# A twelve-layer decoder in one kernel: norm statistics taken in the stage in front, and routed tokens fetched by lists and added by diagonal products

## The chip, the cores and the metric

The kernel runs on one core of a Trainium2 chip, in float32 throughout. The metric is the device time of one execution in microseconds (us), taken as the median of several runs. The engines are TensorE (PE in the profile, its weight loads PEld), VectorE (DVE), ScalarE (ACT), GpSimd (POOL) and SyncE (SP), which here issues most DMAs.

## The reference

A stream x of 16 sequences with 112 tokens of 256 channels passes four layers of three sub-layers each; every sub-layer reads a layer norm of x and is added to x.

```python
m = mean(x); v = var(x); _layernorm = (x - m) / sqrt(v + eps)
x = x + L0_attn(_layernorm(x))         # rwkv-like recurrence
x = x + L0_xattn(_layernorm(x), ctx)   # cross attention, 16 heads, context 375 rows of 192
x = x + L0_ffn(_layernorm(x))          # one dense MLP
x = x + L1_attn(_layernorm(x))         # long convolution, then a second norm and a gated MLP
x = x + L1_xattn(...); x = x + L1_ffn(...)   # 8 experts, two picks per token
x = x + L2_attn(...);  x = x + L2_xattn(..., mask); x = x + L2_ffn(...)  # 8 experts again
x = x + L3_attn(...);  x = x + L3_xattn(...); x = x + L3_ffn(...)        # 4 fixed experts
# the routed one:
topk_val, topk_idx = top_k(logits, 2); scores = softmax(topk_val)
out_e = silu(a) * g @ W2[e] + b2[e]            # for every expert e
out = sum(out_e[topk_idx] * scores)            # over the two picks
```

## The kernel before

x stays on chip as `X` (112 tokens on the partitions, 16 batches of 256 columns, "b" below); `XT` is its normalised transpose. Each sub-layer is a row of blocks, and a block ends when all engines in it have ended, so work of one block does not overlap that of the next, except for what SP has issued. Semaphores order the engines within a block; each engine runs its instructions in the order of the code.

`layer_norm` (L158 on) takes `bn_stats` of eight batches (L206), aggregates them (L209), adds epsilon (L212), lets GpSimd take the power -1/2 (L259), does the same for the other eight, and then VectorE normalises batch by batch (L239), TensorE transposes (L270) and ScalarE copies to `XT`. There is one such norm at the head of each of the twelve sub-layers and a second in L1_attn. The batches of X that it reads were added just before: by `project_out` (L1951, two batches a round), by the attention loop's "O" job (L1369), by `feed_forward` (L417, L419) or by `gather_results` (L987, L989).

`context_attention` (L0_xattn, L1_xattn, L2_xattn) runs a loop over batches and groups of four heads. Between the scores (L1247), the transposes of the probabilities (L1227) and the weighted sums (L1270), TensorE does one "job" at a time, all in PSUM bank 6: per batch K for two column halves (L1189), V for three row tiles (L1199), Q (L1194) and the output O (L1214). The 192 context channels are two chunks of 96 rows. A job waits until VectorE has copied out the one before it.

`sub_l3_xattn` works directly on the context, loading per batch `keys` and `rows` (281 KB each) into three slots; both slots are given free when the batch's weighted sum is done.

A routed MLP: `router` makes the gates; `place_tokens` computes for each token and pick a slot in an array sorted by expert; `add_second_biases` adds the gated second biases to X on VectorE (L569) while GpSimd sends all tokens by 32 indirect DMAs (`scatter_tokens`, L785) to `rows_in` in HBM; `expert_tiles` runs 35 tiles of 128 rows, for each of which SP loads rows (L832), loads the expert's first weights (L837) and stores the result to `rows_out` (L843), TensorE transposes (L872) and multiplies (L884, L893); `gather_results` fetches two rows per token by 32 indirect DMAs (L978), and VectorE multiplies and adds them (L987, L989). At the program's start ScalarE's queue writes zeros over `rows_in`. `KT` is 128, `T` 112, `GB` 4 batches a group, `G` 4 groups, `PICKS` 2.

## Time and profile before

| what | value |
|---|---|
| time, median of 3 runs (range) | 3467.72 us (3465.84 to 3471.27) |
| the profiled execution: its own time, its span | 3473.44 us, 3471.7 us |
| TensorE matmul busy | 2742.4 us, 79% |
| VectorE, ScalarE, GpSimd busy | 1504.5, 1278.5, 870.4 us |
| mean granted TensorE clock | 0.88 |

The sub-layers lie one behind the other. By the windows read from the trace they end at: L0_attn 319, L0_xattn 685, L0_ffn 854, L1_attn 1199, L1_xattn 1620, L1_ffn 1970, L2_attn 2122, L2_xattn 2516, L2_ffn 2922, L3_attn 3094, L3_xattn 3222, L3_ffn 3463 us; then X is stored. A busy share over the whole span says little here; each stage has its own limit, and what is read is which engine waits in it, for what, and how long. In a timeline row, the number in brackets is the engine's idle time before the row and what ended it.

### The profile page before, as it was taken

The numbers are of one execution on the slowest core, as the hardware profiler recorded it, in microseconds if no ns is written. First come the engines' busy times: TensorE is split into PE (matmuls) and PEld (weight loads), VectorE is DVE, ScalarE is ACT, GpSimd is POOL, SyncE is SP. The second block draws the span as 40 slices with busy tenths as digits, with TensorE's granted clock in tenths as the row PEclk, the third lists the DMA queues.
The fourth block names the chain that finished last, engine by engine and source line by source line (L and its number), as shares of the span: only waits on it lengthen the run. The fifth ranks groups of instructions, "written<-read, shape, count | busy, mean of one in ns | idle before, by whom it ended". The sixth has DMA issues, their size and how long they took to land. (4 is left out here: it accounts for less than half of the span.)

```text
span 3471.7 us, 57030 instructions
## 1 busy us (share of the span) xinstructions
PE 2742.4 (79%) x18341; PEld 1973.1 (57%) x18342; DVE 1504.5 (43%) x3582; ACT 1278.5 (37%) x3781; POOL 870.4 (25%) x557
## 2 busy tenths in 40 slices
PE   6554999778786899998399377988848992987798
PEld 2343677545463555554299244666627992865465
DVE  5676888722623333334222484555440004552311
ACT  1322777621531123333022123666613331861111
POOL 2342455400001022222300362444430005320000
PEclk8776999879888999998599687999958996998899
DMA  3000000000330000001276301000035552003000
GB/s 108 1 1 22 17 13 13 6 25 14 77 74 25 33 13 12 12 11 53 84 236 234 108 0 39 12 13 13 5 137 173 181 181 86 1 29 87 26 24 21
DMA packets 116639, 192.75 MB, mean 56 GB/s; under 512 B 57715, under 2 KB 91714, under 8 KB 104754
## 3 DMA queue, kind: packets, MB, share of 16 engines
q1 hardware_dynamic: 105634, 171.84, 15.6%
q0 software_dynamic: 6144, 14.69, 1.4%
q10 hardware_dynamic: 4752, 4.85, 0.4%
q8 instruction: 59, 0.97, 0.1%
q14 instruction: 50, 0.41, 0.0%
HBM read 167.92 MB, written 23.43 MB: 55 GB/s over the span
## 5 line engine op out<-in xcount | busy, mean ns | idle before, releaser
L1177 POOL TENSOR_TENSOR L_xattn_p<-L_xattn_p,L_xattn_ri 112x1500 f32<-112x1500 f32 (+1 forms) x192 | 435.8, 2270 | 655.0 <-DVE L_xattn_ri L1380 655.0
L1307 ACT ACTIVATE L_xattn_pT<-ps 125x448 f32<-125x448 f32 (+1 forms) x576 | 254.9, 476 | 385.6 <-PE ps L1227 385.2
L1319 ACT ACTIVATE L_xattn_p<-L_xattn_sa,L_xattn_ng 112x375 f32<-112x375 f32 x512 | 304.8, 598 | 68.6 <-DVE L_xattn_ng L1409 48.5
L1227 PEld LDWEIGHTS ps<-ident,L_xattn_p 112*125 112x125 f32 x1920 | 259.9, 191 | 88.6 <-issue 19.6
L1227 PE MATMUL ps<-ident,L_xattn_p 112*125 112x112 f32 x1920 | 284.6, 279 | 14.7 <-POOL L_xattn_p L1177 8.8
L270 PE MATMUL ps<-ident,ln_xn 112*128 112x112 f32 x416 | 99.0, 399 | 241.4 <-DVE ln_xn L239 222.9
L884 PE MATMUL ps<-L_ffn_xsT,L_ffn_w 128*128 128x128 f32 x2240 | 267.5, 279 | 11.3 <-issue 10.0
L884 PEld LDWEIGHTS ps<-L_ffn_xsT,L_ffn_w 128*128 128x128 f32 x2240 | 266.6, 195 | 15.9 <-issue 12.5
L259 POOL TENSOR_TENSOR ln_rstd<-ln_tmp,ln_half 112x8 f32<-112x8 f32 x26 | 45.8, 1763 | 793.8 <-DVE ln_tmp L212 602.8
L270 PEld LDWEIGHTS ps<-ident,ln_xn 112*128 112x128 f32 x416 | 67.1, 211 | 274.0 <-issue 246.1
L1199 PE MATMUL ps<-L_xattn_pack,L_xattn_src 97*125 97x256 f32 (+3 forms) x576 | 198.4, 468 | 30.5 <-DVE L_xattn_v L1359 29.9
L1189 PE MATMUL ps<-L_xattn_src,L_xattn_pack 96*128 96x375 f32 x512 | 202.4, 521 | 22.9 <-DVE L_xattn_kT L1340 16.6
L941 DVE COPY L_ffn_y<-ps 128x256 f32<-128x256 f32 x70 | 29.7, 425 | 393.7 <-PE ps L893 393.7
L893 PE MATMUL ps<-L_ffn_weights,L_ffn_hT 128*128 x840 | 192.9, 379 | 2.2 <-DVE L_ffn_hT L952 2.2
L978 POOL DMA_INDIRECT L_ffn_got<-rows_out,slot x64 | 59.9, 935 | 504.7 <-PEq L971 485.8
L1247 PE MATMUL ps<-L_xattn_kT,L_xattn_qm 32*112 32x375 f32 (+1 forms) x1280 | 173.1, 523 | 3.7 <-DVE L_xattn_ng L1406 1.8
L379 PE MATMUL ps<-L_ffn_w,L_ffn_h 128*112 128x256 f32 x768 | 169.0, 379 | 0.0
L367 PE MATMUL ps<-XT,L_ffn_w 128*128 x384 | 151.6, 551 | 20.0 <-DMA L_ffn_w<-in_L_ffn_experts 20.0
L914 ACT ACTIVATE L_ffn_xsT<-ps 128x256 f32<-128x256 f32 x72 | 27.6, 383 | 378.5 <-PE ps L872 378.5
L893 PEld LDWEIGHTS ps<-L_ffn_weights,L_ffn_hT 128*128 128x128 f32 x840 | 154.2, 190 | 20.9 <-issue 2.8
L419 DVE SCALAR_TENSOR_TENSOR X<-ps,L_ffn_gates,X 112x256 f32 x80 | 33.2, 477 | 299.6 <-PE ps L379 299.6
L379 PEld LDWEIGHTS ps<-L_ffn_w,L_ffn_h 128*112 128x112 f32 x768 | 135.9, 177 | 36.0 <-issue 7.7
(378 smaller groups left out, 5069.7 us busy)
## 6 DMA issues: line engine op xcount, KB each, us to landing
L_ffn_w<-in_L_ffn_experts SPq DMA_DIRECT2D x74, 1024.0 KB, 5.1
L_xattn_src<-in_ctx SPq DMA_DIRECT2D x48, 281.2 KB, 2.9
L_attn_toeplitz<-L_attn_h SPq DMA_DIRECT2D x4, 3136.0 KB, 23.4
L_ffn_xs<-rows_in SPq DMA_DIRECT2D x74, 128.0 KB, 2.2
rows_out<-L_ffn_y SPq DMA_DIRECT2D x70, 128.0 KB, 2.3
L_ffn_weights<-in_L_ffn_experts SPq DMA_DIRECT2D x8, 1028.0 KB, 14.7
rows_in<-zeros ACTq DMA_DIRECT2D x1, 4736.0 KB, 27.2
L_xattn_keys<-in_ctx SPq DMA_DIRECT2D x16, 281.2 KB, 3.0
```

What stands on the lines that cost most here:

```text
L270: last = pe.transpose(k.ps[0:KP, u, c * T:(c + 1) * T], xn[:, u, c * KP:(c + 1) * KP], k.ident[0:T, 0:T])
L367: last = pe.matmul(k.ps[0:rows, bank, 0:GT], w1[s][:, c, col:col + rows], src[:, c, bass.ds(g * GT, GT)], start=(c == 0), stop=(c == 1))
L379: last = pe.matmul(k.ps[0:T, 4 + j, 0:D], hT[:, h, m, j * T:(j + 1) * T], w2[s][:, m, :], start=(m == 0), stop=(m == hidden - 1))
L884: last = pe.matmul(k.ps[:, 2 * u + half, j * KT:(j + 1) * KT], w1[:, u, c, at:at + KP], xT[:, u, c, :], start=(c == 0), stop=(c == 1))
L893: last = pe.matmul(k.ps[:, 6 + u, 0:D], hT[:, u, m, :], weights[:, bass.ds(e * rest + (o2 + m * D), D)], start=(m == 0), stop=(m == hidden ...
L1177: g.tensor_tensor(P[:, m % 4, :, :], P[:, m % 4, :, :], ri[:, m % 4, :].unsqueeze(2).broadcast_to([T, W, S2]), ALU.mult).then_inc(s["prob_ ...
L1189: last = pe.matmul(k.ps[:, bank, 0:S2], wk[0:kr, kc, c * KP:(c + 1) * KP], src[0:kr, u, kc, :], start=(kc == 0), stop=(kc == 1))
L1199: last = pe.matmul(k.ps[0:KW, bank, 0:HD], src[0:rows, u, kc, c * KW:(c + 1) * KW], wv[0:rows, kc, :], start=(kc == 0), stop=(kc == 1))
L1227: last = pe.transpose(turned(t)[:, j * T:(j + 1) * T], P[:, m % 4, j, kc * KW:(kc + 1) * KW], k.ident[0:T, 0:T])
L1247: last = pe.matmul(scores(n)[:, j, :], qm[rows, u, e, c, :], KT[rows, u, c, :], start=True, stop=True)
L1307: act.activation(PT[:, m % 4, kc, :, :].rearrange("p h t -> p (h t)"), turned(t), ACT.Copy).then_inc(s["pt_ev_a"].sem, 1)
L1319: last = act.activation(P[:, n % 4, j, :], at, ACT.Exp, bias=ng[:, n % 4, j:j + 1], scale=-1.0 if mask else 1.0, accum_out=rs[:, n % 4, j: ...
```

## The change

Seven parts.

1. `bn_stats` moves out of `layer_norm` into the stage in front: right behind the addition that completes a batch of X, VectorE waits for that addition and takes the batch's statistics into a tile that lives for the whole program. `layer_norm` only aggregates. The first norm takes them as quarters of X land. The dense MLPs, all attentions and the gather do so; L3_ffn, the last, has no norm behind it.
2. The routed MLPs no longer scatter. The normalised tokens are written once, in order, to `rows_x`; `add_second_biases` also computes on VectorE and TensorE, for every tile, the list of its rows; GpSimd fetches each tile's rows by list from `rows_x` and sends its results by list to `rows_y`, where they lie by token and pick. SP loads weights alone.
3. The gather becomes eight plain DMAs of 448 KB on the queues of SP and ScalarE. ScalarE makes, ahead of the tiles, 32 diagonal matrices `shares` from the picks' weights; TensorE multiplies each fetched block by its matrix and sums the two picks in PSUM; VectorE adds the sums to X, two batches at a time.
4. In L2_xattn the context is laid out as 128 rows and 64 rows, the 64 held twice. K's two halves form one job, V's tiles 0 and 1 form one, V's tile 2 is made in two column halves: the 64-row products of each pair lie in two different row groups of TensorE. A batch has five jobs, not seven, and a pair fills banks 6 and 7.
5. L3_xattn has four slots for `keys`, free when the scores are done, and five for `rows`.
6. X is stored in four quarters, each when its last addition is done.
7. X is loaded in four quarters and the first weights are issued right behind them; 3712 KB of zeros are written, not 4736.

```diff
+    def moments(self, v, b, of=None):
+        of = self.X if of is None else of
+        return v.bn_stats(self.st[:, bass.ds(6 * b, 6)], of[:, bass.ds(b * D, D)])
...
@@ project_out, behind the two additions of a round @@
+                    for u in range(2):
+                        b = 2 * i + u
+                        v.wait_ge(*s["res_done"].at(b + 1))
+                        k.moments(v, b, of=out)
...
@@ add_second_biases @@
+                def list_rows(c):
+                    pe.wait_ge(*s["rg_hot"].at(c + 1))
+                    for n in range(c * part, (c + 1) * part):
+                        last = pe.matmul(k.ps[0:KT, 6, 0:2 * (most - 1)], place[:, n, :],
+                                         owned[:, n, :, :].rearrange("p w q -> p (w q)"), start=(n == 0),
+                                         stop=(n == picks - 1))
...
@@ expert_tiles @@
-                        load(t + 2, 1 - u)
-                        load_first(t + 2, 1 - u)
-                        store(t - 1, u)
+                        load_first(2 * i + u + 3, 1 - u)
...
+                def fetch(t):
+                    g.wait_ge(*s["rg_turned"].at(t - 1))
+                    g.indirect_dma_start(xs[:, t % 2, :], None, k.rows_x[:, :],
+                                         bass.IndirectOffsetOnAxis(ap=route.rows[:, 0, t:t + 1], axis=0)).then_inc(
+                                             x_in[t % 2].sem, 16)
+                def send(t):
+                    g.wait_ge(*s["rg_y"].at(t + 1))
+                    g.indirect_dma_start(k.rows_y[:, :],
+                                         bass.IndirectOffsetOnAxis(ap=route.rows[:, 1, t:t + 1], axis=0),
+                                         y[:, t % 2, :], None).then_inc(y_out[t % 2].sem, 16)
+                for t in range(NT):
+                    if t + 2 <= NT:
+                        fetch(t + 2)
+                    if t > 0:
+                        send(t - 1)
...
+                for n in range(PICKS):
+                    for b in range(B):
+                        act.activation(shares[:, n, b, :], k.ident[0:T, 0:T], ACT.Copy,
+                                       scale=route.weight[:, n, b:b + 1])
...
@@ gather_results, with parts = 8 and per = 2 @@
-                    for n in range(PICKS):
-                        g.indirect_dma_start(got[:, b % ring, n * D:(n + 1) * D], None, rows[:, :],
+                    eng.dma_start(got[:, q * per:(q + 1) * per, :, :], rows[:, q * per:(q + 1) * per, :, :]).then_inc(
+                        into[q % 4].sem, 16)
...
+                            last = pe.matmul(k.ps[0:T, q % 4, u * D:(u + 1) * D], shares[:, n, q * per + u, :],
+                                             got[:, q * per + u, n, :], start=(n == 0), stop=(n == PICKS - 1))
...
+                    v.tensor_tensor(x, k.ps[0:T, q % 4, 0:per * D], x, ALU.add).then_inc(s["rg_added"].sem, 1)
+                    if q > 0:
+                        look(q - 1)
...
@@ context_attention @@
+    if paired:
+        places = {(0, "a"): ("K", 0), (0, "b"): ("V", 2), (1, "a"): ("O", 0), (1, "b"): ("Q", 0), (3, "b"): ("V", 0)}
...
+                if kind == "K" and paired:
+                    for c in range(C):
+                        pe.matmul(k.ps[:, bank + c, 0:S2], wk[:, 0, c * KP:(c + 1) * KP], src[:, u, 0, :], start=True,
+                                  stop=False)
+                    for c in range(C):
+                        rows = slice(64 * c, 64 * c + 64)
+                        last = pe.matmul(k.ps[:, bank + c, 0:S2], wk[rows, 1, c * KP:(c + 1) * KP], src[rows, u, 1, :],
+                                         start=False, stop=True)
...
@@ sub_l3_xattn @@
-    SLOTS = 3
+    KS, RS = 4, 5
...
-                sp.wait_ge(*summed.at(b - SLOTS + 1))
-                load(sp, b)
+                sp.wait_ge(*scored.at(b - KS + 1))
+                load_keys(sp, b)
+                if b + 1 < B:
+                    sp.wait_ge(*summed.at(b + 1 - RS + 1))
+                    load_rows(sp, b + 1)
```

How instructions stand now. First VectorE in the round of `project_out` in L0_attn, before: `po_x` is the product that the next round's transposes need, `X<-ps,X` one batch's addition; an ISA row is a wait or a signal.

```order
L2275 ISA
L2275 TENSOR_TENSOR po_x<-L_attn_V,L_attn_G 112x256
L1949 ISA
L1951 ISA
L1951 TENSOR_TENSOR X<-ps,X 112x256
L1949 REGISTER_ALU
L1951 ISA
L1951 TENSOR_TENSOR X<-ps,X 112x256
L1932 REGISTER_ALU
```

The same place in the changed kernel.

```order
L2501 ISA
L2501 TENSOR_TENSOR po_x<-L_attn_V,L_attn_G 112x256
L2171 ISA
L2173 ISA
L2173 TENSOR_TENSOR X<-ps,X 112x256
L2171 REGISTER_ALU
L2173 ISA
L2173 TENSOR_TENSOR X<-ps,X 112x256
L122 ISA
L122 BN_STATS st<-X 112x6
L122 ISA
L122 BN_STATS st<-X 112x6
```

Two waits and two statistics now stand at the round's end, in front of the next round's `po_x`.

Second, TensorE in the loop of L2_xattn, before: a K job (L1189), transposes of probabilities (L1227), the other K job.

```order
L1189 MATMUL ps<-L_xattn_src,L_xattn_pack 128x375 x2
L1224 REGISTER_ALU
L1225 REGISTER_ALU
L1227 MATMUL ps<-ident,L_xattn_p 125x112 x4
L1225 REGISTER_ALU
L1227 MATMUL ps<-ident,L_xattn_p 125x112 x4
L1208 REGISTER_ALU
L1189 MATMUL ps<-L_xattn_src,L_xattn_pack 128x375 x2
```

And now: L1330 is the pair's 128-row products, L1334 its two 64-row products in two row groups, L1340 and L1344 the same of V's tile 2 by column halves.

```order
L1330 MATMUL ps<-L_xattn_src,L_xattn_pack 128x375 x2
L1334 MATMUL ps<-L_xattn_src,L_xattn_pack 128x375 x2
L1390 REGISTER_ALU
L1391 REGISTER_ALU
L1393 MATMUL ps<-ident,L_xattn_p 125x112 x4
L1391 REGISTER_ALU
L1393 MATMUL ps<-ident,L_xattn_p 125x112 x4
L1369 REGISTER_ALU
L1340 MATMUL ps<-L_xattn_pack,L_xattn_src 125x128 x2
L1344 MATMUL ps<-L_xattn_pack,L_xattn_src 125x128 x2
```

Both K halves stand in the first job, and V's tile 2 took the place of the second.

Third, VectorE in the routed MLP between `place_tokens` and the tiles, before.

```order
L772 CAST expert<-owner 1x37
L696 UNCONDITIONAL_BRANCH
L564 UNCONDITIONAL_BRANCH
L566 COPY gates_in_order<-L_ffn_gates 112x128
L569 TENSOR_TENSOR X<-ps,X 112x512 x8
L537 UNCONDITIONAL_BRANCH
```

And now: `past`, `rest` and `owned` mark each token's tile and id, `place` its row in the tile; `rows` is the list.

```order
L641 COPY gates_in_order<-L_ffn_gates 112x128
L621 TENSOR_TENSOR past<-pick,L_ffn_pack 112x1184
L623 TENSOR_REDUCE rest<-past 112x32
L624 TENSOR_SCALAR rest<-rest 112x32
L625 TENSOR_TENSOR rest<-rest,pick 112x32
L626 TENSOR_TENSOR past<-past 112x32x36
L616 TENSOR_TENSOR X<-ps,X 112x512 x2
L631 TENSOR_TENSOR owned<-past,L_ffn_pack 112x32x36 x2
L637 TENSOR_TENSOR place<-rest,L_ffn_pack 112x1024
...
L657 SCALAR_TENSOR_TENSOR spare<-ps,L_ffn_pack 128x36
L658 CAST rows<-ps 128x36
L659 TENSOR_TENSOR rows<-ps,spare 128x36
```

The additions of the second biases stand between the steps of the list, and the tiles' first fetch comes behind all of it.

## Rows read from the trace of the kernel before

**Rows 1.** Windows by stage: length; busy PE, PEld, DVE, ACT, POOL; clock; DMA share, GB/s.

```profile
322.00:687.50 365.50, 328.17 (x3360) 242.01 (x3360) 290.17 (x436) 257.74 (x739) 186.73 (x71) 0.96 0.06 16
...
2122.00:2518.00 396.00, 331.38 (x3360) 244.38 (x3360) 206.40 (x779) 257.72 (x740) 178.88 (x68) 0.95 0.06 17
...
3096.00:3224.00 128.00, 92.67 (x448) 66.38 (x448) 39.73 (x120) 27.47 (x90) 5.67 (x4) 0.86 0.28 78
```

**Rows 2.** Timeline where one sub-layer ends and the next begins (start, duration).

```profile
2120.48 1.42 DVE L417 TENSOR_TENSOR X<-ps,X 112x256 f32 x4 [5.06 <-PE ps L379]
...
2122.43 2.71 DVE L206 BATCH_NORM_STATS2 ln_st<-X 112x6 f32<-112x256 f32 x8
...
2126.10 1.65 POOL L259 TENSOR_TENSOR ln_rstd<-ln_tmp,ln_half 112x8 f32<-112x8 f32 x1 [40.47 <-DVE ln_tmp L212]
...
2129.43 3.62 DVE L239 TENSOR_SCALAR ln_xn<-X,ln_mv,ln_rstd 112x256 f32<-112x256 f32 x7
```

**Rows 3.** Timeline of TensorE in the output projection of L0_attn.

```profile
299.22 0.74 PE L1967 MATMUL ps<-ident,po_x 112*128 112x112 f32 x4 [1.25 <-DVE po_x L2275]
...
302.98 0.74 PE L1967 MATMUL ps<-ident,po_x 112*128 112x112 f32 x4 [1.24 <-DVE po_x L2275]
```

**Rows 4.** Timeline of TensorE in L2_xattn, one batch.

```profile
2325.32 1.13 PE L1199 MATMUL ps<-L_xattn_pack,L_xattn_src 96*125 96x256 f32 x4 [1.19 <-DVE L_xattn_v L1359]
...
2326.80 0.90 PE L1247 MATMUL ps<-L_xattn_kT,L_xattn_qm 32*112 32x375 f32 x8
...
2331.20 1.53 PE L1189 MATMUL ps<-L_xattn_src,L_xattn_pack 96*128 96x375 f32 x4 [1.18 <-DVE L_xattn_kT L1340]
...
2337.86 1.14 PE L1194 MATMUL ps<-XT,L_xattn_pack 128*128 x8 [0.68 <-DVE X L1369]
...
2347.85 1.13 PE L1199 MATMUL ps<-L_xattn_pack,L_xattn_src 96*125 96x256 f32 x4 [1.19 <-DVE L_xattn_v L1359]
```

**Rows 5.** Waits in L3_xattn, and the window over its 16 batches.

```profile
PE ps L1808 <- DMA L_xattn_keys<-in_ctx: 20.4, 11, 2.7
...
3117.60:3221.50 103.90, 80.59 (x392) 57.50 (x392) 24.34 (x64) 20.23 (x70) 0.00 (x0) 0.90 0.26 73
```

**Rows 6.** Timeline in L1_ffn, between routing and the first tile.

```profile
1673.28 0.27 DVE L566 COPY gates_in_order<-L_ffn_gates 112x128 f32<-112x128 f32 x1 [0.39 <-PEq L696]
...
1718.76 0.69 PE L872 MATMUL ps<-ident,L_ffn_xs 128*128 128x128 f32 x2 [28.09 <-remote]
...
1719.34 0.34 SPq L837 DMA_DIRECT2D L_ffn_w<-in_L_ffn_experts  x1
...
1724.55 2.26 PE L884 MATMUL ps<-L_ffn_xsT,L_ffn_w 128*128 128x128 f32 x9 [5.10 <-issue]
```

**Rows 7.** VectorE on 4096 elements a partition (timeline, L0_attn).

```profile
283.30 4.42 DVE L2259 TENSOR_TENSOR L_attn_V<-L_attn_V,L_attn_gw 112x4096 f32<-112x4096 f32 x1
```

**Rows 8.** Windows of L1_ffn: its tile loop, and its gather.

```profile
1719.00:1928.00 209.00, 197.45 (x1472) 188.73 (x1471) 54.28 (x175) 54.97 (x177) 0.06 (x1) 0.97 0.68 230
...
1928.00:1973.00 45.00, 0.00 (x0) 0.00 (x0) 18.00 (x41) 0.20 (x1) 29.80 (x32) 0.51 0.32 90
```

**Rows 9.** Timeline of L1_ffn's gather.

```profile
1924.40 0.42 DVE L941 COPY L_ffn_y<-ps 128x256 f32<-128x256 f32 x1 [2.17 <-PE ps L893]
...
1927.94 0.96 POOL L978 DMA_INDIRECT L_ffn_got<-rows_out,slot  x1 [214.06 <-PEq L971]
...
1969.56 0.48 DVE L989 SCALAR_TENSOR_TENSOR X<-L_ffn_got,weight,X 112x256 f32<-112x256 f32 x1
```

**Rows 10.** DMA issues: count, size of one, median time to landing.

```profile
L_ffn_w<-in_L_ffn_experts SPq DMA_DIRECT2D x74, 1024.0 KB, 5.1
...
L_ffn_xs<-rows_in SPq DMA_DIRECT2D x74, 128.0 KB, 2.2
...
X<-in_x SPq DMA_DIRECT2D x1, 1792.0 KB, 10.4
...
out<-X SPq DMA_DIRECT2D x1, 1792.0 KB, 7.9
```

More of the change, by code:

```diff
@@ L176, in layer_norm @@
         tmp = sb("ln_tmp", [T, B])
-        half = sb("ln_half", [T, B])
         xn = sb("ln_xn", [T, 4, D])
@@ L292, in layer_norm, with feed_forward @@
                   rstd_done=4 if two_pows else 2, norm_done=B, norm_tr=B, norm_ev=B)
-def feed_forward(k, name, dram, layout, experts, rows, hidden, gated, act_fn, gates=None, src=None):
+def feed_forward(k, name, dram, layout, experts, rows, hidden, gated, act_fn, gates=None, src=None, out=None):
     nc = k.nc
@@ new lines, in own_rows, with places @@
+                def own_rows():
+                    for w in range(2):
+                        last = v.tensor_tensor(owned[:, :, w, :], past[:, :, 0:most - 1],
+                                               along(ids[:, w * picks:(w + 1) * picks], most - 1), ALU.mult)
+                    ch.link(last)
+                def places(c):
+                    at = slice(c * part, (c + 1) * part)
+                    v.tensor_tensor(place[:, at, :], along(rest[:, at], KT),
+                                    ranks.unsqueeze(1).broadcast_to([T, part, KT]), ALU.is_equal).then_inc(
+                                        s["rg_hot"].sem, 1)
@@ L590, in sub_ffn @@
     elay, edram = packs[name + "_experts"]
-    feed_forward(k, name, edram, elay, spec["experts"], KP, spec["hidden"], spec["gated"], spec["act"], gates)
+    feed_forward(k, name, edram, elay, spec["experts"], KP, spec["hidden"], spec["gated"], spec["act"], gates,
+                 out=k.aps["out"] if spec["mode"] == "fixed" else None)
 def fixed_gates(k, gates, b2):
@@ L995, in sub_routed_ffn @@
+                look(parts - 1)
+        k.advance(rg_added=parts, rg_summed=parts, **{f"rg_got{r}": 32 for r in range(4)})
 def sub_routed_ffn(k, ctx, name, packs, spec):
@@ L1369, in job @@
                     v.tensor_tensor(k.x(b - 2), k.ps[0:T, 6, 0:D], k.x(b - 2), ALU.add).then_inc(job_out.sem, 1)
+                    v.wait_ge(*job_out.at(count))
+                    k.moments(v, b - 2)
+                    return
+                if paired and (kind, c) == order[J_V]:
+                    v.wait_ge(*s["pv_mm"].at((b - 1) * (UB // E)))
+                    store(kind, c, u, 6)
                     return
@@ L3148, in _ @@
             def _(v):
+                v.memset(k.half[:, :], -0.5)
                 v.memset(routed_zeros[:, :], 0.0).then_inc(k["vec_step"].sem, 1)
```

431 lines of the change are left out of this document (292 added, 139 removed).

## The prediction

> **What bounds the kernel now.** I read the windows by sub-layer first. TensorE has the largest busy share in every stage [rows 1], but not all of it: L2_xattn spends 331 of 396 us in products, L3_xattn 93 of 128. So the question in each stage is what TensorE waits for, and I went on to timelines where it stands still. Four kinds of gaps show.
>
> At each sub-layer's start nothing runs but VectorE: the first statistics begin at 2122.43 and the first normalised batch at 2129.43, 7.0 us later [rows 2]. GpSimd's power had ended at 2127.75; VectorE was then still at the statistics of the second eight batches. Inside L2_xattn, TensorE waits three times a batch for VectorE to clear PSUM bank 6: 1.19, 1.18 and 0.68 us of a period of 22.5 [rows 4]. In L3_xattn it waits 11 times for the context, 20.4 us [rows 5]. In a routed MLP it stands still from the router to the first tile (the scatter, 28 us) and again for the whole gather [rows 6, 8, 9]. In between, the tile loop is full: PE is busy 197 of 209 us at a clock of 0.97 [rows 8].
>
> **The change part by part.** *Statistics (part 1).* The norm's statistics leave its head. What stays before the first normalised batch is the aggregation and epsilon (from the end of the statistics at 2125.14 to the power's start at 2126.10, 0.96 us), the power (1.65) and about 0.1 of handover: 2.7 instead of 7.1 with the memset that goes too, so 4.4 us are saved [rows 2]. There are 13 norms; the first is counted below, 12 give 52.8 us. What they cost in front: one statistic is 2.71 / 8 = 0.34 us, with its wait for the addition 0.44. Behind a stage's last addition stand one in the four cross attentions (0.5), four in the three dense MLPs (1.5), two in three output projections (0.8): 2 + 4.5 + 2.4 = 8.9 us. Inside the stages, `project_out` is a chain: TensorE's transposes wait 1.25 us for `po_x`, which VectorE makes behind the two additions, and the period is 302.98 - 299.22 = 3.76 us [rows 3]. The order now puts two waits and two statistics in front of that `po_x`, about 0.75 us in each of 7 rounds: 5.2 us in L0_attn and 5.2 in L1_attn; in L3_attn I count nothing, as that projection lies in a loop with many more products per batch; if it is a chain too, it is 5.2 more, which the lower bound has room for. In L0_xattn VectorE is busy 290 of 365 us [rows 1], so statistics in front of a maximum may delay the softmax; 16 times 0.44 is 7 us at worst, nothing at best; I take 2. Sum 52.8 - 8.9 - 10.4 - 2 = **32 us**. Bounds: 20 (L0_xattn's 7 in full, and 0.5 at every other stage's rounds) and 42 (project_out's share hidden).
>
> *Pairs in L2_xattn (part 4).* A K job of four instructions takes 1.53 us, a V job 1.13 [rows 4]; 3.06 and 3.39 a batch. Of a K pair's eight instructions four are 64-row ones which can run two at a time, so a quarter of the time goes; V's likewise: 0.77 + 0.85 = 1.6 us, and as records overlap their successors a little I take 1.4. That groups of rows do run together is seen in the scores: eight instructions of 375 columns on 32 rows take 0.90 us, where four of 375 columns take 1.53 [rows 4]. The handovers of bank 6 go from seven to five. The wait between V's last two jobs (1.19) has no successor, since V's tile 2 has gone to the other end; the one behind K stays (1.18) and may grow by one copy of 0.55, as the pair has two banks to copy out. So 0.6 to 1.2 us of waits go. Together 2.0 to 2.6, times 16: **35 us**. Bounds 15 (only the matmul time, and that less what follows under the rivals) and 45.
>
> The Trainium skill, page "TensorEngine Tiling (Array Packing)", Key Properties, says that tiles in different row groups work in parallel, with which the row of the scores agrees, but also that changing the tiling mode drains the engine, which speaks against this part. What a change of mode can cost at most is in the same row: ideal for the eight score instructions, at 1.53 / 4 = 0.38 each and four at a time, is 0.77 us; the row has 0.90, so 0.13 remain for a change. The change adds six of these a batch, 0.8 us, 12 us in all.
>
> *L3_xattn (part 5).* Keys are now asked for when a batch's scores are done, four batches ahead, and no longer after the weighted sum of three batches ago. A load of 281 KB is short against a batch's cycle of (103.9 - 25) / 16 = 4.9 us, so the 20.4 us of waits should go. The granted clock of those 104 us was 0.90 [rows 5]: a fifth of the time, 21 us, stood at the lower of its two levels (1.2 of 2.4 GHz), which costs half of it, 10 us; about half of that falls into the waits themselves, so I count 5 more. **25 us**, bounds 14 (the DMAs go on being late every other time) and 29.
>
> *Routed MLPs (parts 2 and 3), twice.* Before, 51.3 us lie between the copy of the gates (1673.28) and the first product (1724.55) [rows 6]. Now the list ends the block. VectorE works through 2 x 1184 + 1152 + 2 x 1152 + 4 x 1024 = 9920 elements a partition (marks and sum, differences, ids, places), at 4.42 us for 4096, or 1.08 ns each [rows 7], 10.7 us; the eight additions of biases are 512 elements from PSUM, 5.3 us; small ones and waits 2; the last list products and the list itself some 3. That makes 21 us. Behind it come a block change (0.4), the fetch (0.96 to issue [rows 9], 2.2 to land [rows 10]), and the first weights, 5.1 us from their issue, as before 1719.34 to 1724.55 [rows 6, 10]: with the diagonal matrices' 32 small copies on ScalarE (estimated at 0.22 us each, 7 us) beside them, the first product at about 29.2. That saves 22.1 us. If VectorE's broadcast operands cost double, 12 less; if the matrices push the first tile, 3 less. The gather before runs from 1924.40 to the end of the last addition at 1970.04, 45.6 us [rows 9], most of it the pitch of GpSimd's issues. Now: copy 0.4, last send 3.3, block change 0.4, 3584 KB at the rate of the output's store (1792 KB in 7.9 us, of which about 2 are fixed [rows 10]), 14 us; the last block's four products, addition and two statistics 3.3. That makes 21.5; I take 22 saved of the possible 24. At the rate of the input's load (10.4 us [rows 10]) it would be 19.4 us of transfer and 18.5 saved. The tile loop I take as unchanged, since TensorE fills it [rows 8]; GpSimd needs two issues of some 1.2 us a tile of 5.5. Both routed MLPs have this code before and after the tiles, so 2 x (22.1 + 22) = **88 us**, bounds 65 and 100.
>
> *Ends (parts 6 and 7).* Instead of 7.9 us for the whole store one quarter remains, (7.9 - 2) / 4 + 2 = 3.5: 4.4 us. The start gains 2: its statistics overlap with the landing of X, but the weights then bound it.
>
> **Sum**: 32 + 35 + 25 + 88 + 4.4 + 2 = 186 us. The profiled execution took 3473.4 us, the median is 5.7 lower; 3473.4 - 186 = 3287, and for the median 3467.7 - 186 = 3282.
>
> **The rivals.** (a) *The lists slow the tiles.* Each tile's rows come by GpSimd's queue, the fetch of one behind the send of another, and TensorE waits at the transposes. For it: in all 32 issues of the old gather GpSimd managed one in 1.24 us. Against: a fetch is asked for two tiles before it is used, 11 us, and needs 3.2. At 1 us a tile for 70 tiles the time is 3282 + 70 = 3352. Chance 0.08. (b) *Pairing and statistics give little*: the 12 us of mode changes, the copy behind the K pair in full, and statistics that delay the maxima in L2_xattn too. Then part 4 gives 15 and part 1 20: 3282 + 20 + 12 = 3314. For it: TensorE already waits for VectorE in just that loop. Chance 0.14. (c) *The plain gather runs no faster per byte than the indirect one*, whose window shows 90 GB/s and a DMA share of 0.32 [rows 8]: 41 us instead of 14 a gather, and 3282 + 54 = 3336. Against: the low rate goes with the issues' pitch. Chance 0.06. (d) *Slower than before*: the fetch needs more than its 11 us. It decides from 186 / 70 = 2.7 us a tile, so 13.7 us from request to landing, over four times the rows' 3.2; at 16 us the time is 3282 + 5 x 70 = 3632. Nothing speaks for it but that the trace has no indirect fetch beside full weight traffic (DMA share 0.68). Chance 0.02. (e) *More than I count*: the granted clock, 0.86 in L3_xattn and 0.90 in its loop [rows 1, 5], lies between its two levels wherever TensorE had stood idle, and may rise at more places than L3_xattn as gaps close: some 30 us, 3250. Chance 0.10. My forecast has 0.60.
>
> **The numbers.** The independent errors (about 11, 13, 7 and 17 us of the four large parts) make 25 us around 3282 for the likeliest case; with (b) and (e) within and most of (a) and (d) without, 3246 to 3330. A measurement of this kernel tells about 0.2%, 7 us. All cases but (d) are faster by far: 0.97, and 0.01 for no change.
>
> **What would show it.** Right: first normalised batch 2.7 us after a norm's block begins; no wait for `keys`; first tile product about 29 us behind the gates' copy; from the last tile's copy to the next norm 22 us; the L2_xattn period 20.2 us; project_out's period 4.5. Wrong: a wait of TensorE for `xs` in the tile loop, a period over 21 us in L2_xattn with its waits for VectorE grown, or a list block over 25 us.

## The result

| kernel | median, us | ratio to before, 95% interval |
|---|---|---|
| before | 3468.26 | |
| changed | 3344.91 | 0.9644 (0.9627 to 0.9660) |

The change takes 123 us off, 3.6%. I had forecast 186 and a range of 3246 to 3330; the time lies above it. The page of the changed kernel begins:

```profile
span 3343.8 us, 57353 instructions
...
PE 2799.0 (84%) x18661; PEld 1999.5 (60%) x18662; DVE 1519.8 (45%) x3568; ACT 1294.2 (39%) x3845; POOL 888.0 (27%) x570
```
The profiled spans differ by 127.9 us. Cut at the first normalised batch of each norm, they fall to the stages so (worked out from the timelines of both; a stage holds the head of the next norm):

| stage | before | changed | difference | forecast |
|---|---|---|---|---|
| to the first norm | 24.3 | 27.0 | +2.8 | -2 |
| L0_attn | 302.4 | 308.6 | +6.2 | +1.6 |
| L0_xattn | 365.6 | 368.2 | +2.7 | -1.9 |
| L0_ffn, L1_attn | 514.1 | 507.5 | -6.6 | -4.2 |
| L1_xattn | 421.5 | 415.8 | -5.6 | -3.9 |
| L1_ffn, L2_ffn | 756.6 | 696.6 | -60.0 | -96.8 |
| L2_attn, L3_attn | 323.5 | 315.7 | -7.8 | -6.5 |
| L2_xattn | 393.5 | 368.1 | -25.4 | -38.9 |
| L3_xattn | 127.7 | 99.9 | -27.8 | -28.9 |
| L3_ffn and the store | 242.5 | 236.2 | -6.3 | -4.4 |

(The forecast column is the prediction's terms, each norm's 4.4 us less its tail put to the stage in front.) The forecasts sum to -186, the spans to -128. Of the missing 58 us 37 are in the two routed MLPs; the rest is in L2_xattn, L0_attn, L0_xattn and the start.

**What came as forecast.** The head of a norm, here L3_xattn's, in the timeline of the changed kernel:

```profile
3004.20 0.43 DVE L122 BATCH_NORM_STATS2 st<-X 112x6 f32<-112x256 f32 x1
...
3005.01 0.64 DVE L217 BATCH_NORM_AGGREGATE ln_mv<-st 112x2 f32<-112x6 f32 x8 [0.38 <-PEq L1697]
...
3005.93 3.44 POOL L267 TENSOR_TENSOR ln_rstd<-ln_tmp,half 112x8 f32<-112x8 f32 x2 [9.22 <-DVE ln_tmp L220]
...
3007.62 4.71 DVE L247 TENSOR_SCALAR ln_xn<-X,ln_mv,ln_rstd 112x256 f32<-112x256 f32 x7 [1.02 <-POOL ln_rstd L267]
```
The statistics of the last batch (L122) end before the block; aggregation, power and first normalised batch follow each other, 2.6 us where [rows 2] has 7.0. L3_xattn's waits for keys are gone, and its stage is 28 us shorter where I had said 29. The store at the end is one quarter.

**Start.** The timeline of the changed kernel:

```profile
7.54 11.96 ACTq L3385 DMA_DIRECT2D rows_x<-zeros  x1
...
19.97 0.35 SPq L198 DMA_DIRECT2D L_attn_pack<-in_L_attn  x1
...
27.02 3.29 DVE L247 TENSOR_SCALAR ln_xn<-X,ln_mv,ln_rstd 112x256 f32<-112x256 f32 x9
```
ScalarE's second DMA issue, one row of zeros, takes 12.0 us, behind the 3712 KB that it issued at 7.06. The block ends with it: SP issues the next one's first DMA at 19.97. X's statistics, meant to overlap with its landing, begin only then.

**L0_attn's projection.** VectorE's product, TensorE's transposes and the window of the changed kernel:

```profile
297.51 0.76 DVE L2501 TENSOR_TENSOR po_x<-L_attn_V,L_attn_G 112x256 f32 x2
...
298.07 0.74 PE L2193 MATMUL ps<-ident,po_x 112*128 112x112 f32 x4 [1.86 <-DVE po_x L2501]
...
303.23 0.76 DVE L2501 TENSOR_TENSOR po_x<-L_attn_V,L_attn_G 112x256 f32 x2
...
290.30:332.90 42.60, 29.34 (x96) 19.71 (x96) 18.10 (x48) 5.92 (x17) 0.00 (x0) 0.70 0.00 0
```
And the same projection in the kernel before:

```profile
288.30:319.50 31.20, 21.98 (x96) 15.00 (x96) 12.94 (x32) 5.92 (x18) 0.00 (x0) 0.92 0.00 0
```
TensorE waits 1.86 us for `po_x`, 0.6 more than in [rows 3]. The round that starts at 297.51 ends at 303.23, 5.7 us and not 4.5; of the five rounds behind the first two, one (303.23 to 307.60) takes 4.4 us, the others 5.6 to 6.2, and the eight product records in them take 3.0 to 3.6 us together, not 2.0. The projection takes 42.6 us after 31.2, 11.4 more where I had 6.0, and the granted clock over it is 0.70 after 0.92: the other 5.4 us are the clock. In L1_attn's projection, the same loop, a round takes 4.11 us after 3.54 and TensorE waits 1.69 us after 1.12, and there the clock of the rounds stays at 1.00. So longer waits went with a lower clock in L0_attn (1.82 to 1.86 us of 4.4) and not in L1_attn (1.69 of 4.1); what lies between the two, no run here tells.

**L2_xattn.** TensorE in the changed kernel:

```profile
2275.69 1.13 PE L1340 MATMUL ps<-L_xattn_pack,L_xattn_src 128*125 128x256 f32 x4
...
2276.75 0.70 PE L1344 MATMUL ps<-L_xattn_pack,L_xattn_src 64*125 64x256 f32 x4
...
2278.83 1.53 PE L1330 MATMUL ps<-L_xattn_src,L_xattn_pack 128*128 128x375 f32 x4
...
2280.28 0.90 PE L1334 MATMUL ps<-L_xattn_src,L_xattn_pack 64*128 64x375 f32 x4
...
2281.11 1.13 PE L1393 MATMUL ps<-ident,L_xattn_p 112*125 112x112 f32 x8
...
2282.85 0.70 PE L1340 MATMUL ps<-L_xattn_pack,L_xattn_src 128*125 128x128 f32 x4 [0.61 <-DVE L_xattn_kT L1518]
...
2283.48 0.49 PE L1344 MATMUL ps<-L_xattn_pack,L_xattn_src 64*125 64x128 f32 x4
...
2246.47 1.14 PE L1355 MATMUL ps<-XT,L_xattn_pack 128*128 x8 [0.68 <-DVE X L1560]
...
2267.93 1.14 PE L1355 MATMUL ps<-XT,L_xattn_pack 128*128 x8 [0.66 <-DVE X L1560]
```
From Q job to Q job it is 21.5 us after 22.5 [rows 4]; I had forecast 20.2. K's pair is 1.53 + 0.90 = 2.43 us after 3.06, V's tiles 0 and 1 are 1.13 + 0.70 = 1.83 after 2.26. But tile 2 in halves of 128 columns is 0.70 + 0.49 = 1.19 us after 1.13. And the transposes of the probabilities got slower, in the groups by line over 12 batches, changed kernel first, then before.

```profile
L1393 PE MATMUL ps<-ident,L_xattn_p 112*125 112x112 f32 x575 | 84.9, 283 | 4.2 <-ACT L_xattn_pT L1475 4.2
```

```profile
L1227 PE MATMUL ps<-ident,L_xattn_p 112*125 112x112 f32 x576 | 78.8, 273 | 0.0
```
They cost 6.1 us more in 12 batches, 0.5 a batch: eight of them take 1.13 us behind 64-row products (2281.11) and 1.02 behind the 96-row ones of before. That is three of the five groups that got slower; the other two stand where a job has gone, one behind the scores and one behind a wait. TensorE's busy time over 12 batches is 236.1 of 257.5 us after 234.7 of 270.3: it did not fall at all. Records overlap, so the sizes are better read from start to start. A K job of the kernel before is 1.37 us long by that:

```profile
2327.63 1.53 PE L1189 MATMUL ps<-L_xattn_src,L_xattn_pack 96*128 96x375 f32 x4
...
2329.00 1.02 PE L1227 MATMUL ps<-ident,L_xattn_p 112*125 112x112 f32 x8
```
Two of them took 2.74 us, and the pair takes 2.28 (2278.83 to 2281.11). All five jobs of a batch took 5.55 us, and the three pairs take 5.03. These 0.5 us are what the transposes give back. TensorE's waits fell, for bank 6 and the like from 35.4 to 22.1 us, 1.1 us a batch, and that is the whole gain.

**The lists and the first tile**, L1_ffn of the changed kernel, and the window of its lists' block:

```profile
1672.61 0.27 DVE L641 COPY gates_in_order<-L_ffn_gates 112x128 f32<-112x128 f32 x1 [0.38 <-PEq L789]
...
1684.33 3.69 PE L582 MATMUL ps<-owned,place 112*128 112x72 f32 x16 [1.16 <-DVE place L637]
...
1706.41 0.18 DVE L659 TENSOR_TENSOR rows<-ps,spare 128x36 int32<-128x36 f32 x1
...
1708.43 1.20 POOL L937 DMA_INDIRECT L_ffn_xs<-rows_x,rows  x1 [48.85 <-issue]
...
1716.05 0.69 PE L967 MATMUL ps<-ident,L_ffn_xs 128*128 128x128 f32 x2 [10.02 <-DMA L_ffn_xs<-rows_x,rows]
...
1717.21 0.93 PEld L979 LDWEIGHTS ps<-L_ffn_xsT,L_ffn_w 128*128 128x128 f32 x4 [0.88 <-ACT L_ffn_xsT L1009]
...
1672.60:1705.00 32.40, 30.91 (x109) 24.21 (x109) 17.18 (x20) 2.13 (x4) 0.00 (x0) 0.50 0.00 1
```
From the gates' copy to the list it is 34.0 us (I had 21), to the first tile product 44.6 (I had 29.2; before, 51.3 [rows 6]). VectorE is busy 17 of 32 us, as costed; TensorE is busy 31 of them, at a granted clock of 0.50, the lower level of 1.2 GHz, from end to end. In L2_ffn it is the same, 34.0 and 44.4 us. Then the first fetch takes from 1708.43 to 1716.05 to be used, 7.6 us and not 3.2. The tile loop itself, from the first tile product to the last result's copy, takes 199.5 us after 199.9.

**The gather**, same place:

```profile
1920.32 8.86 SPq L1078 DMA_DIRECT2D L_ffn_got<-rows_y  x4
...
1925.80 16.44 PE L1098 MATMUL ps<-L_ffn_got,L_ffn_shares 112*112 112x256 f32 x64 [9.16 <-DMA L_ffn_got<-rows_y]
...
1942.88 1.39 DVE L122 BATCH_NORM_STATS2 st<-X 112x6 f32<-112x256 f32 x4
...
1944.65 0.64 DVE L217 BATCH_NORM_AGGREGATE ln_mv<-st 112x2 f32<-112x6 f32 x8 [0.37 <-PEq L1072]
```
From the last result's copy (1916.67) to the next norm it is 28.0 us after 46.2 (1924.40 [rows 9] to the next norm's first statistics at 1970.58); I had 21.5. The loads took about 16 us (their DMA share is 1.13 to 1.14 until 1935). TensorE's 64 instructions, of which I had counted only the last eight, take 16.4 us and begin 5.5 us behind the loads' issue, at a clock of 0.50 until 1930.

### The profile page after: what moved, and what is told of

Its sections match the earlier page's. It is cut to its first block and busy times, and to the rows that moved or that the text cites. A ratio compares the mean times of both kernels' runs of the same rounds, so it can differ in the third digit from the quotient of the medians.

```text
span 3343.8 us, 57353 instructions
## 1 busy us (share of the span) xinstructions
PE 2799.0 (84%) x18661; PEld 1999.5 (60%) x18662; DVE 1519.8 (45%) x3568; ACT 1294.2 (39%) x3845; POOL 888.0 (27%) x570
## 3 DMA queue, kind: packets, MB, share of 16 engines
q8 instruction: 62, 1.02, 0.1%
## 5 line engine op out<-in xcount | busy, mean ns | idle before, releaser
L1393 PEld LDWEIGHTS ps<-ident,L_xattn_p 112*125 112x125 f32 x1920 | 253.1, 190 | 115.4 <-ACT L_xattn_pT L1475 35.4
L1393 PE MATMUL ps<-ident,L_xattn_p 112*125 112x112 f32 x1920 | 294.7, 284 | 21.2 <-ACT L_xattn_pT L1475 11.3
L267 POOL TENSOR_TENSOR ln_rstd<-ln_tmp,half 112x8 f32<-112x8 f32 x26 | 44.3, 1720 | 785.4 <-DVE ln_tmp L220 596.3
L411 ACT ACTIVATE L_ffn_h<-ps,L_ffn_w 128x448 f32<-128x448 f32 x96 | 60.8, 633 | 251.2 <-PE ps L382 251.2
L1360 PE MATMUL ps<-L_xattn_pack,L_xattn_src 96*125 96x256 f32 (+3 forms) x384 | 145.9, 503 | 11.7 <-DVE L_xattn_v L1550 11.1
L1350 PE MATMUL ps<-L_xattn_src,L_xattn_pack 96*128 96x375 f32 x384 | 147.4, 508 | 6.1 <-DVE L_xattn_kT L1528 2.1
L943 POOL DMA_INDIRECT rows_y<-L_ffn_y,rows x70 | 69.2, 988 | 293.8 <-DVE L_ffn_y L1041 287.3
```

The source lines that it names most:

```text
L1350: last = pe.matmul(k.ps[:, bank, 0:S2], wk[0:kr, kc, c * KP:(c + 1) * KP], src[0:kr, u, kc, :], start=(kc == 0), stop=(kc == 1))
L1360: last = pe.matmul(k.ps[0:KW, bank, 0:HD], src[0:rows, u, kc, c * KW:(c + 1) * KW], wv[0:rows, kc, :], start=(kc == 0), stop=(kc == 1))
L1393: last = pe.transpose(turned(t)[:, j * T:(j + 1) * T], P[:, m % 4, j, kc * KW:(kc + 1) * KW], k.ident[0:T, 0:T])
```

## The experiments

Ratios are to the kernel before on the same chip, with their intervals; "us" is the difference to the changed kernel's 0.9644, at 3468 us. Those intervals are some 6 us wide to either side, so a difference of two ratios under about 8 us is not told from nothing. "Stage" numbers are from the profiled executions, one each, cut as in the table above. Stages that an edit leaves alone differ from profile to profile: L0_attn 305.2 to 310.6 us, L1_attn's first part 190.2 to 195.0, L0_xattn 366.7 to 372.5, L1_ffn 318.1 to 320.1, the others by 1 to 3 us.

**Statistics back in the norms** (e1). `layer_norm` takes `bn_stats` as before, all `moments` in front are gone.

```diff
-                    if x_in is not None:
-                        for b in range(h * HB, (h + 1) * HB):
+                    for b in range(h * HB, (h + 1) * HB):
...
-                            last = k.moments(v, b)
+                        last = k.moments(v, b, of=src)
...
-                    v.wait_ge(*job_out.at(count))
-                    k.moments(v, b - 2)
```

> All statistics are back at the head of each norm (part 1 undone; the other parts stay; the waits for a batch's own addition go too). Theory from the two traces: each of 12 norms gets 4.4 us longer (53), and the stages in front get back what the statistics cost there: about 10 us in L0_attn, 5 in L1_attn, 5 to 7 in L0_xattn, 7 of tails elsewhere. Part 1 is then worth some 26 us: 3371. My prediction's term of 32 would give 3377. Rival, that the statistics cost in front as much as they give behind: 3345.

Ratio 0.9689 (0.9673 to 0.9705), +16 us; the profiled span is 24 longer. Part 1 is worth 16 to 24 us. By stages: L0_attn is 6.6 us shorter without it, L0_xattn 2.8 and L3_xattn 1.4; L1_attn, L2_attn, L3_attn, L1_xattn, L2_xattn and the MLPs that have a norm behind them are 2 to 5.4 longer each. In L0_xattn the norm behind the stage accounts for 4.4 us the other way, so the 16 statistics in that loop cost about 2.8 + 4.4 = 7.2 us, near my upper bound; with this stage's scatter it is anything from 5.6 to 11.5.

**Statistics one round later in project_out** (e5).

```diff
+                begin(0)
+                begin(1)
+                finish(0)
+                with v.Fori(1, B // 2 - 1) as i:
+                    begin(i + 1)
+                    look(i - 1)
+                    finish(i)
...
```

> In project_out VectorE takes a round's two statistics one round later, behind the next round's po_x and ahead of the additions, where it waits for products anyhow; nothing else changes. Theory: the 0.75 us a round were on the chain because they stood ahead of po_x, and in L0_attn they also let the granted clock fall (0.69 over the projection, 0.90 before). Both go: L0_attn 8 us shorter, L1_attn's first part 4, so 3346 - 12 = 3334. Rival, that the chain runs through the additions in any place: no change.

Ratio 0.9627 (0.9607 to 0.9648), -6 us, within the intervals; the profiled span is 12.0 shorter. The stages are plain: L0_attn is 9.0 us shorter, L1_attn's first part 4.9, both below every profile with the old place. TensorE in L0_attn:

```profile
302.79 0.74 PE L2204 MATMUL ps<-ident,po_x 112*128 112x112 f32 x4 [1.29 <-DVE po_x L2512]
...
306.57 0.74 PE L2204 MATMUL ps<-ident,po_x 112*128 112x112 f32 x4 [1.26 <-DVE po_x L2512]
...
290.00:324.50 34.50, 22.16 (x96) 15.15 (x96) 20.26 (x58) 6.12 (x18) 0.00 (x0) 0.89 0.00 0
```
The wait is 1.29 us as before the change, the period 3.78, the clock 0.89; in L1_attn the round is back at 3.54 us. From the first `po_x` to the next norm's first instruction on VectorE the projection of L0_attn takes 31.6 us, where it was 42.6 in the changed kernel and 31.3 before. The statistics' place, not their length, cost what the two stages gained here, some 14 us give or take their scatter.

**Statistics behind the maxima in the attentions** (e6): the pair of `wait_ge` and `moments` goes to the end of the step.

> In the three context attentions VectorE takes the statistics of an O job at the end of its step, behind the maxima and the step's other jobs, and no longer between the addition and the maxima. Theory: L0_xattn loses its 4 to 5 us, 3341; L1_xattn and L2_xattn within 1 us of before. Rival, that L0_xattn is full on VectorE, and 16 times 0.43 us cost the same anywhere: 3346.

Ratio 0.9635 (0.9618 to 0.9653), -3 us, which the intervals don't tell from nothing. The stage tells a little more: L0_xattn took 365.6 us here, and 361.3 and 362.9 in e11 and e14b, which have other edits too; in eleven profiles with the changed kernel's order it took 366.7 to 372.5. So the edit gains something there, 1 to 7 us by this run; the scatter allows no closer figure.

**The small DMA first** (e4): the issue for `rows_x` stands ahead of the one for `rows_y`.

> At the start ScalarE issues the small DMA (one row of zeros to rows_x) before the large one, not behind it. In the changed kernel the second issue kept ScalarE for 12.0 us and with it the block until 19.97. Theory: the block ends at about 8, statistics run as X lands, and the first normalised batch comes at 18 to 21 instead of 27; the weights' load then bounds L0_attn's start, so 5 to 7 us of the time, 3339. Rival, that the DMA engines are full with X and zeros and nothing comes earlier: 3345.

Ratio 0.9623 (0.9606 to 0.9639), -7 us, at the edge of what the intervals tell. The timeline is plain:

```profile
7.05 0.51 ACTq L3382 DMA_DIRECT2D rows_x<-zeros  x1
...
7.60 0.42 ACTq L3383 DMA_DIRECT2D rows_y<-zeros  x1
...
20.45 5.84 DVE L247 TENSOR_SCALAR ln_xn<-X,ln_mv,ln_rstd 112x256 f32<-112x256 f32 x16
```
Both issues now take 0.5 us, and the first normalised batch comes 6.6 us earlier. L0_attn is 1.2 us longer, which is less than its scatter.

**L2_xattn unpaired** (e2) and **paired in one row group** (e12).

```diff
-    paired = mask
+    paired = False
...
@@ e12, for K, and the same for V @@
-                        rows = slice(64 * c, 64 * c + 64)
+                        rows = slice(0, 64)
```

> L2_xattn alone goes back to seven jobs a batch and 96-row products (part 4 undone). By the trace of the changed kernel a batch takes 21.1 us instead of 22.5, so 16 batches cost 22 us more: 3367. The prediction's term (35) would give 3380; the rival that pairing saves only matmul time, 0.65 us a batch, and no waits, 3355.

> In L2_xattn both 64-row products of a pair read rows 0 to 63, one row group (the 64 channels stand there twice, so the result is the same). Theory: in the changed kernel they overlap almost fully, at 0.83 us for K's four instructions against 1.45 us for the four of 128 rows; one behind the other they take 1.4 to 1.5 us, so K + 0.6, V tiles 0 and 1 + 0.4, V tile 2 + 0.2 per batch, times 16: 3346 + 19 = 3365. Rival, that what they gain is the handover and not the overlap: 3350.

e2: 0.9697 (0.9681 to 0.9714), +18 us, its stage 17.9 longer. e12: 0.9696 (0.9680 to 0.9712), +18 us, its stage 15.2 longer. TensorE of e12, K's pair:

```profile
2267.05 1.53 PE L1330 MATMUL ps<-L_xattn_src,L_xattn_pack 128*128 128x375 f32 x4
...
2268.50 1.52 PE L1334 MATMUL ps<-L_xattn_src,L_xattn_pack 64*128 64x375 f32 x4
```
In one row group the four 64-row instructions take 1.52 us, as long as four of 128 rows; in two they take 0.90 (above), of an ideal of 0.76. The overlap is worth 15.2 us, 0.95 us a batch; without it 2.7 of the 17.9 us of stage time are left, which the whole times don't tell from nothing.

The Trainium skill, "TensorEngine Tiling (Array Packing)", Key Properties, says both that tiles work in parallel and that a change of mode drains the engine. The trace agrees with the first (1.52 against 0.90), and fits the second. The starts of single instructions show what a change costs. Products of 375 columns follow each other every 0.315 us, of 128 rows as of 64 in e12; from the last one of 128 rows to the first of 64 it is 0.41, and from that to the next 0.42. Behind the 64-row products it is the same: 0.09 us more up to the first transpose, and 0.20 from it to the second, where 0.10 to 0.11 is usual. So each change of row count costs 0.09 + 0.10 = 0.19 us, in e12 without any overlap as in the changed kernel with it, and in the kernel before wherever TensorE leaves the 32-row scores. It is not a cost of 64-row products as such, since in e12 they run at the pace of the others behind the first. Two transposes behind a wait, when TensorE was empty, also start 0.20 us apart, which fits a drain.

The six changes that the pairs add are then 1.1 us a batch, 18 in the stage, and not the 0.8 and 12 that the prediction gave to rival (b): its row of the scores holds only the half of a change that falls inside the group. Without them the three pairs would take 4.15 us where the five jobs took 5.55, just the 1.4 us that the prediction counted; this last is worked out, no run removes the changes alone.

**L3_xattn with three slots** (e3).

```diff
-    KS, RS = 4, 5
+    KS, RS = 3, 3
...
-                sp.wait_ge(*scored.at(b - KS + 1))
+                sp.wait_ge(*summed.at(b - KS + 1))
```

> L3_xattn has three slots for keys and rows again, both free after the weighted sum (part 5 undone). Theory: the 20 us of waits for keys and the slower clock behind them come back, 3345 + 25 = 3370. Rival, that the load time and not the slots made the waits: no more than 5 us, 3350.

Ratio 0.9726 (0.9710 to 0.9742), +28 us; the stage is 28.6 longer, and the waits (here for eight of the batches, in the window up to 3110 us) are back:

```profile
PE ps L2021 <- DMA L_xattn_keys<-in_ctx: 14.7, 8, 2.7
```

**TensorE warmed up for the lists** (e7). In `place_tokens`, nine products whose result nobody reads:

```diff
+                for _ in range(9):
+                    pe.matmul(k.ps[:, 7, 0:512], k.ident[:, :], k.XT[:, 0, 0:512], start=True, stop=True)
```

> During place_tokens, where TensorE has nothing to do for 11 us, it runs nine products of 128 rows and 512 columns into a bank that nobody reads; the lists' block behind it is unchanged. Theory A: the list block (34 us) is bound by TensorE at the lower clock (granted 0.50 throughout, busy 31 of 32 us), because it had stood idle before; started at the full clock it halves until VectorE's 20 us bound it: 14 us saved in each routed MLP, 3318. Theory B: the small products (8 rows, or 72 columns) don't hold the clock, it is back at 0.50 within a few us, and no more than 3 us are saved each time: 3341.

Ratio 0.9653 (0.9635 to 0.9670), no difference. Windows of the lists' block:

```profile
1672.00:1676.00 4.00, 2.40 (x20) 1.95 (x21) 3.48 (x6) 1.80 (x4) 0.00 (x0) 1.00 0.00 0
...
1676.00:1680.00 4.00, 2.23 (x9) 1.47 (x8) 3.86 (x7) 0.00 (x0) 0.00 (x0) 0.83 0.01 2
...
1685.00:1690.00 5.00, 5.00 (x17) 4.03 (x17) 1.23 (x2) 0.00 (x0) 0.00 (x0) 0.50 0.00 0
```
The block starts at the full clock (1.00), but is back at 0.50 within 8 us, in which TensorE is busy 4.6 us, and stays there while TensorE is busy 5.00 of 5 us. Theory A is wrong: standing idle before is not what keeps the clock low. With this block's products, of 8 rows or of 72 columns, it doesn't come up again, though TensorE is full; in the gather, with products of 112 rows and 256 columns, it rises from 0.50 to 1.00 within some 5 us. Which trait of the products decides, no run here separates.

**Less, and other, work on TensorE in the lists' block** (e9, e13b). e9 moves the gates' transposes and four of eight pairs of bias products into `place_tokens`; e13b on top makes the other four ahead of the list products, while VectorE marks.

```diff
-                for c in range(4):
-                    if route is not None:
-                        list_rows(c)
-                    if c < 2:
-                        biases(4 + 2 * c)
-                        biases(5 + 2 * c)
+                for i in range(4, 8):
+                    biases(i)
+                for c in range(4 if route is not None else 0):
+                    list_rows(c)
```

> The gates' transposes, their copies and the first four of eight pairs of bias products (24 of TensorE's instructions and their clock-bound 10.3 us) move from the lists' block forward into place_tokens, where TensorE has nothing to do for 11 us; the additions stay in the lists' block. Theory: that block is bound by TensorE at the lower clock, so it gets 9 to 10 us shorter in each routed MLP: 3346 - 19 = 3327. Rival, VectorE's chain of marks and places bounds it at about 30 us: at most 3 us each, 3340.

> On e9_early_bias: in the lists' block VectorE first adds the four pairs of biases that are ready, then makes marks and places; TensorE makes the other four pairs of bias products (7.4 us) under the marks and then the list products without a break. Theory: the block is the sum of VectorE's head (the trace of e9: 9.8 us, now with 1.3 more) and of TensorE's work behind the first place; with 7.5 us of that moved under the head, the block takes 11 + 14.8 + 0.5 = 26 us instead of 32 in e9: 3344 - 12 = 3332. Rival, VectorE's places pace TensorE and nothing is gained: 3344.

e9: 0.9632 (0.9614 to 0.9650), -4 us, within the intervals; each routed MLP 3 us shorter, the lists' block 32.1 us after 34.0. The number is the rival's, but neither engine alone bounds the block: with 10 us of work gone, TensorE stood still for 11.5 us at the block's head, waiting for VectorE's first place, and then did 22 us of products in a row. e13b: 0.9602 (0.9578 to 0.9625), -15 us; each routed MLP 8 to 10 us shorter than in the changed kernel, the block 25.5 us (26 expected). Its trace:

```profile
1681.13 13.73 PEld L584 LDWEIGHTS ps<-owned,place 112*128 112x128 f32 x64 [3.79 <-DVE place L638]
...
1695.44 0.18 DVE L660 TENSOR_TENSOR rows<-ps,spare 128x36 int32<-128x36 f32 x1
```
All list products run in one piece, 13.9 us, and end the block. So the block's length is VectorE's chain up to the first place plus TensorE's work that stands behind it, at the lower clock.

**First weights and matrices early** (e10): SP issues the first two expert loads and ScalarE makes the 32 matrices in the lists' block.

> The first two loads of expert weights (SP) and the diagonal matrices (ScalarE) are made in the lists' block, where both are idle, and not at the head of the tiles. Theory: the first fetch took 7.6 us to land because two loads of 1 MB were issued just ahead of it; alone it lands 3 us after its issue, and neither weights nor matrices (9.0 us on ScalarE) stand in the way: first product 4 to 5 us earlier in each, 3337. Rival, an indirect fetch from HBM takes 7 us by itself: the matrices' 0.5 us only, 3345.

Ratio 0.9615 (0.9599 to 0.9631), -10 us; each routed MLP 3.8 to 5.6 us shorter.

```profile
1708.86 1.20 POOL L941 DMA_INDIRECT L_ffn_xs<-rows_x,rows  x1 [48.87 <-issue]
...
1712.62 0.69 PE L971 MATMUL ps<-ident,L_ffn_xs 128*128 128x128 f32 x2 [6.16 <-DMA L_ffn_xs<-rows_x,rows]
```
From issue to use it is 3.8 us after 7.6. The fetch had landed late because two loads of 1 MB stood in front of it; ScalarE's 9.0 us for the matrices (I had estimated 7) ended at 1716.64, just before they would have mattered.

**The gather's arithmetic on VectorE** (e8): plain loads stay, and two multiply-adds a batch, as before the change, take the place of TensorE's products and VectorE's addition.

> The gather's plain loads stay; VectorE weights and adds the two picks by two multiply-adds a batch as before the change, and TensorE does nothing there (ScalarE still makes the diagonal matrices, unused). VectorE then has 4 x 0.52 + 0.74 = 2.8 us a part of two batches, eight parts 22.6, against 1.73 us a part of TensorE's products. Theory: the products bound the gather now, VectorE would bound it more; 5 us longer in each routed MLP, 3356. Rival, that the loads bound it and the products are hidden: 3346 either way.

Ratio 0.9657 (0.9640 to 0.9674), no difference; L1_ffn 1.5 us shorter, L2_ffn 0.7 longer, both within the scatter, and from the last result's copy to the next norm 28.0 us again. My theory, 5 us more in each, was wrong:

```profile
1923.33 0.88 DVE L1107 SCALAR_TENSOR_TENSOR X<-L_ffn_got,weight,X 112x256 f32<-112x256 f32 x2 [8.23 <-DMA L_ffn_got<-rows_y]
...
1940.92 1.40 DVE L122 BATCH_NORM_STATS2 st<-X 112x6 f32<-112x256 f32 x4
```
A multiply-add costs 0.44 us in a pair, not 0.52, and VectorE starts 5.0 us behind the loads' issue, where TensorE's sums reach VectorE 9.3 behind it. 19 us of VectorE and 16.4 + 2.4 of TensorE and its tail come to the same. So in the gather the plain loads made the gain; the diagonal products neither add to it nor take from it.

**All together** (e11, e14b). The edits of e4, e5, e6, e9 and e10, and three 512-column products at the gather's head; e14b with the order of e13b.

> The edits together: statistics of project_out one round later, those of the attentions behind the maxima, the small DMA of zeros first, biases and weights and matrices early, and three products of 512 columns at the head of the gather, for the clock. The sum of the parts as measured or expected: 11 + 4 + 5.6 + 19 + 9 + 3 = 52, so 3294.

> The same order on top of e11_all (3302). By the theory of e13b 12 us less, 3290; by its rival 3302.

e11: 3301.9 us, 0.9518 (0.9498 to 0.9538), 8 above what I expected, since 19 us stood in that sum for e9, which gave 4. The products at the gather's head do what e7's could not: the clock is at 0.96 when the sums begin, and from the last result's copy to the next norm it is 25.5 us after 28.0. e14b: 3290.6 us, 0.9486 (0.9469 to 0.9503), 54 us below the changed kernel and 178 below before. Of the 63 us that the change fell short of the forecast, changes of place and order, with the three products added at each gather's head, bring back 54.

## Why the prediction was wrong, step by step

- *Heads of the norms, 52.8 us*: right (2.6 us where 7.1 stood).
- *What statistics cost in front*: mis-sized. project_out was seen as a chain, and its 0.75 us a round were right (0.6 in L1_attn), but I held the clock fixed; in L0_attn it went from 0.92 to 0.70 with the longer waits, and came back with them (0.89, e5), 11.4 us and not 6.0. In L0_xattn I took 2 of 0 to 7 us; it was about 7 (e1). Part 1 is 16 to 24 us, forecast 32.
- *Pairs in L2_xattn, 35 us*: mis-sized, 18 (e2). The step is the 1.4 us a batch of matmul time: the sum put the six changes of row count at nothing, though the prediction had read a price for them. They take 1.1 us, and with two more groups of transposes slowed TensorE's busy time stayed as it was. The waits fell by 1.1 us, as forecast (0.6 to 1.2). Rival (b) had 15 us for this part, near in number and partly by luck: its changes are there, larger than it said, but what is left is the waits, which it had cut too.
- *L3_xattn, 25 us*: right, 28.
- *The list block, 21 us*: the step that failed. "VectorE works through" 9920 elements: that sum was right, 17 us busy, but I added up VectorE alone. TensorE's 16 transposes, 16 bias products and 32 list products stand in the same chain, at half the clock. A window of the kernel before that I had not read shows TensorE busy 17 of the 20 us behind the gates' copy, at 0.50:

```profile
1673.00:1693.00 20.00, 17.07 (x48) 11.40 (x48) 5.80 (x9) 2.13 (x4) 14.35 (x15) 0.50 0.26 80
```
That was 13 us too few, twice; e9 and e13b show the chain. Behind the list I had 8.2 us up to the first tile product, a figure that the prediction's rows don't quite add up to; it was 10.6.
- *The fetch, 3.2 us*: 7.6, behind the weights; I took durations of single transfers and did not ask what was issued just ahead (e10). That is 4 us twice, of which 2.4 show in the first product's time, since the weights had been forecast to come later than the rows.
- *The gather, 22 saved*: 18. The loads were near, 14 us forecast, 16 measured. TensorE's products were counted for the last block only, at the full clock.
- *Start, gain 2*: a loss of 2.8. I looked at the DMA engines and not at the issuing queue: one more small DMA behind a large one held ScalarE, and a block with it, for 12 us (e4).
- *Rivals*: (a), (c) and (d) did not happen; the tile loop runs as before, TensorE full, and the plain loads take 16 us and not 41. Both amounts of (b) were near, 15 and 20 us against 18 and 16 to 24, and still its 3314 is 31 us short, because no case had the lists' block. The sum of all parts had the right sign everywhere but at the start and in L0_xattn; the size was off by a third because each term took the engine that I had looked at as the one that sets the stage.

What stays open: how much of L0_xattn's 7 us a later place of the statistics gets back, why a change of row count costs what it does, which trait of a product lets the clock rise, and what the lists' block would take at the full clock, since nothing tried kept it there.

## What to carry to other kernels

When work moves into a block, add up every engine's instructions there, at the clock that the rows of that very block show, and follow the chain between them; the engine with the new work need not be the one that ends it. Where a cheap instruction is put into a loop that is a chain, its place counts and not its length: behind the instruction that the other engine waits for it was free. A price that was read from a row belongs into the sum, and not only into a rival. And for each new DMA ask what its queue and its engines hold at that moment, both when it is a large one in front of a small one and when it is two in front of the one that is waited for.

## What the hardware showed that I had not expected

- An issue of one row behind 3712 KB kept ScalarE for 12.0 us; issued first, 0.5 us.
- In the lists' block, with products of 8 rows or 72 columns, the granted clock fell from 1.00 to 0.50 within some 8 us (e7) and stayed there with TensorE busy 5.00 of 5 us; in e13b it was 0.50 through 14 us of 72-column products with TensorE busy 13.9 of them. In the gather, with products of 112 rows by 256 columns, it rose.
- Four 64-row instructions in one row group take as long as four of 128 rows (1.52 and 1.53 us); in two groups 0.90.
- Eight transposes behind 64-row or 32-row products take 1.12 to 1.13 us, behind 96-row products 1.02. By the starts, each change between 128, 64 and 32 rows costs 0.19 us, overlapped or not.
